# First expert stage of a two-layer MoE kernel: row gathers paced by their own landings, and TensorE waiting tile by tile

## What is computed

```
x = x + 0.5 * ffn(layernorm(x))      # 8 experts, top 2, 1,024 slots per expert
x = x + attention(layernorm(x))      # 16 heads of 8, linear attention with elu+1
x = x + 0.5 * ffn(layernorm(x))      # the same weights again

def ffn(x):
    scores = softmax(x @ wg); topv, topi = top_k(scores, 2)
    disp[topi, pos] = x                      # rows to the slots of their experts, at most 1,024 each
    h = relu(disp @ w1 + b1); y = h @ w2 + b2    # 128 -> 512 -> 128 for each expert
    return sum_k gate_k * y[topi_k, pos_k]
```

## Time and profile before

| | |
|---|---|
| median of 3 runs | 514.09 us |
| lowest, highest | 510.62, 518.35 us |
| the profiled execution | 502.3 us |
| its span, first to last instruction | 500.6 us |
| mean granted TensorE clock in it | 0.848 |
| PE busy | 350.9 us (70%) |
| DVE busy | 354.0 us (71%) |
| POOL busy | 272.6 us (54%) |
| gathers of the first expert stage | 64, from 50.1 to 147.1 us |

### The profile page before, as it was taken

The page is one execution under the profiler, slowest core; times in us unless marked ns, Lnnn a source line. Parts: engine busy times, 40 slices in busy tenths (PEclk is TensorE's granted clock), DMA queues, the critical chain, the costliest instruction groups (busy, mean ns, idle before and its releaser), DMA issues.

```text
span 500.6 us, 6027 instructions
## 1 busy us (share of the span) xinstructions
PE 350.9 (70%) x1710; PEld 286.2 (57%) x1710; DVE 354.0 (71%) x1084; ACT 235.4 (47%) x431; POOL 272.6 (54%) x302
## 2 busy tenths in 40 slices
PE   6913589999999256869777684000789999999400
PEld 6903368888887135748665563000768888888300
DVE  6898379998887545779886586300068989999573
ACT  3687156766666044453642543200057766666200
POOL 8000766766653556666666356777303677777720
PEclk9999999999999867795775896555689999999955
DMA  8930315676663411111111011111401223321489
GB/s 233 353 109 1 111 43 194 196 228 222 211 215 128 126 43 42 43 44 42 45 49 48 29 37 54 53 56 56 163 9 50 87 89 90 91 61 43 139 316 284
DMA packets 45216, 55.48 MB, mean 111 GB/s; under 512 B 6694, under 2 KB 28736, under 8 KB 45184
## 3 DMA queue, kind: packets, MB, share of 16 engines
q1 hardware_dynamic: 32304, 35.40, 21.4%
q0 software_dynamic: 8512, 17.60, 12.1%
q10 hardware_dynamic: 4368, 2.10, 1.4%
HBM read 25.98 MB, written 29.10 MB: 110 GB/s over the span
## 4 chain that ended last, share of the span: by engine, by line
PE 40%; POOL 17%; DMA 12%; issue 11%; DVE 6%; another core or an unknown queue 2%; ACT 1%; POOLq 0%; DVEq 0%; SPq 0%; ACTq 0%
POOL xs_dram L838 8%; DMA yg<-y_dram,slot 6%; PE psum L1041 5%; PE psum L1054 5%; PE psum L1037 5%; PE psum L1052 5%; PE psum L1053 5%; POOL yt_dram L996 5%; PE psum L1038 5%; POOL xg L1010 3%; PE psum L1063 2%; PE psum L1024 2%; DMA ring<-yt_dram 2%; POOL yg L1250 2%
## 5 line engine op out<-in xcount | busy, mean ns | idle before, releaser
L1104 ACT ACTIVATE hf<-psum,bcol 128x512 f32<-128x512 f32 x128 | 88.4, 693 | 65.2 <-PE psum L1041 42.0
L1010 POOL DMA_INDIRECT xg<-xn_dram,gidx x64 | 66.3, 1035 | 68.8 <-POOLq L1671 38.2
L996 POOL DMA_INDIRECT yt_dram<-y_sb,target x64 | 71.6, 1119 | 53.3 <-DVE y_sb L1157 30.9
L1141 DVE TENSOR_TENSOR hl<-hf,hh 128x512 fp32r<-128x512 f32 x128 | 87.8, 698 | 5.0 <-ACT hh L1106 1.4
L1250 POOL DMA_INDIRECT yg<-y_dram,slot x64 | 61.5, 961 | 48.6 <-DMA yg<-y_dram,slot 24.0
L838 POOL DMA_INDIRECT xs_dram<-xns,place x64 | 62.2, 971 | 35.0 <-issue 19.3
L1130 DVE TENSOR_TENSOR xl<-psum,xh 128x512 fp32r<-128x512 f32 x32 | 21.9, 683 | 51.8 <-ACT xh L1089 51.8
L1037 PE MATMUL psum<-xh,wres 128*128 128x512 f32 x128 | 54.0, 422 | 3.8 <-ACT xh L1089 3.8
L1052 PE MATMUL psum<-hh,wres 128*128 128x512 f32 x128 | 52.8, 412 | 0.0
L1041 PE MATMUL psum<-xl,wres 128*128 128x512 f32 x128 | 51.6, 403 | 0.8 <-DVE xl L1130 0.7
L1038 PE MATMUL psum<-xh,wres 128*128 128x512 f32 x128 | 51.2, 400 | 0.0
(11 more groups left out here) (239 smaller groups left out, 751.6 us busy)
## 6 DMA issues: line engine op xcount, KB each, us to landing
yt_dram<-zeros SPq DMA_DIRECT2D x24, 256.0 KB
ring<-yt_dram SPq DMA_DIRECT2D x24, 256.0 KB
xs_dram<-zeros SPq DMA_DIRECT2D x16, 288.0 KB
xg<-xs_dram SPq DMA_DIRECT2D x16, 288.0 KB
wexp_raw<-in_L_ffn_w SPq DMA_DIRECT2D x16, 256.0 KB, 6.0
y_dram<-y_rows_out SPq DMA_DIRECT2D x16, 256.0 KB
x_sb<-in_L_attn_x SPq DMA_DIRECT2D x8, 256.0 KB, 3.9
xn_dram<-xns SPq DMA_DIRECT2D x8, 256.0 KB, 5.8
```

What stands on the lines that cost most here:

```text
L996: gp.indirect_dma_start(out=yt_dram, out_offset=bass.IndirectOffsetOnAxis(ap=target[:, j:j + 1], axis=0), in_=self.y_sb[:, s % YG, t], in_ ...
L1010: gp.indirect_dma_start(out=self.xg[:, s % 4, t], out_offset=None, in_=xn_dram, in_offset=bass.IndirectOffsetOnAxis(ap=gidx[:, j:j + 1], a ...
L1104: one = nc.scalar.activation(self.hf[:, c], bank[1 + c][:], ACT.Relu, bias=bcol[:, at:at + 1])
L1141: dve.tensor_tensor(self.hl[:, s % 2, c], self.hf[:, c], self.hh[:, s % 2, c].bitcast(F32), ALU.subtract).then_inc(hl_ready[c], 1)
```

## The change

Two edits in `Experts`, both for the first expert stage only:

- POOL: gather number i (i = 4s + t) no longer waits for PE's products. From i = 2 on it waits for the landing of gather i - 2. From chunk 4 on, the first gather of a chunk waits before that for `xT_ready >= s - 3`, which says that PE has transposed chunk s - 4 and its buffer is free. Each gather counts on the semaphore of its tile number, `gathered[t]`, no longer on that of its buffer.
- PE: the first transpose of a chunk waits for tile 0, and each of the other three for its own tile.

Everything else (the order of the instructions on every engine, the buffers, the stores and zero fills of SP) stays as it is.

```diff
             def gpsimd(self, gp):
                 for s in range(NSB):
+                    if s >= 4:
+                        gp.wait_ge(xT_ready, s - 3)
                     for t in range(GT):
-                        if s == 2 and t == 0:
-                            gp.wait_ge(xT_ready, 1)
-                        elif s == 2:
-                            gp.wait_ge(h_ready[t - 1], 1)
-                        elif s >= 3:
-                            older, c = divmod(HC * (s - 3) + 2 + t, HC)
-                            gp.wait_ge(h_ready[c], older + 1)
+                        i = GT * s + t
+                        if i >= NARROW:
+                            gp.wait_ge(gathered[(i - NARROW) % GT], landings(i - NARROW))
                         j = GT * self.order[s] + t
                         gp.indirect_dma_start(out=self.xg[:, s % 4, t], out_offset=None, in_=xn_dram,
-                                              in_offset=bass.IndirectOffsetOnAxis(ap=gidx[:, j:j + 1], axis=0)).then_inc(gathered[s % 4], 16)
+                                              in_offset=bass.IndirectOffsetOnAxis(ap=gidx[:, j:j + 1], axis=0)).then_inc(gathered[t], 16)
 
             def tensor(self, pe):
                 b = self.b
 
                 def turn(s):
                     if self.f == 0:
-                        pe.wait_ge(gathered[s % 4], 64 * (s // 4 + 1))
+                        pe.wait_ge(gathered[0], landings(GT * s))
                     else:
                         pe.wait_ge(slot_rows_in[s % XG], 16 * (s // XG + 1))
                     if b + s > 0:
                         pe.wait_ge(xl_ready, b + s)
                     for t in range(GT):
+                        if self.f == 0 and t > 0:
+                            pe.wait_ge(gathered[t], landings(GT * s + t))
                         last = nc.tensor.transpose(bank[0][:, t * P:(t + 1) * P], self.xg[:, s % (4 if self.f == 0 else XG), t, 0:C], ident[:])
                     last.then_inc(xT_ready, 1)
```

## The result

| | before | changed |
|---|---|---|
| first measurement, median (range, runs) | 512.23 us (506.31 to 518.35, 6) | 519.66 us (514.16 to 526.33, 6) |
| first measurement, ratio | | 1.034, 95% interval 1.024 to 1.043 |
| again, on a chip whose runs lie closer together | 490.55 us (486.7 to 492.94, 11) | 506.27 us (505.68 to 508.0, 6) |
| again, ratio | | 1.033, 95% interval 1.029 to 1.037 |
| span of a profiled execution | 500.6 us | 512.4 us; again 504.3 us |

The kernel became slower, by 3.3% or 15.7 us in the second measurement, which is the closer one and the one I rely on. I had forecast +6 us (1.3%), so the difference is two to three times the forecast. That the predicted absolute time of 520 us lies on the first measurement's median is luck: the runs there spread over 12 us for either kernel, and the two medians differ by 7.4 us only.

What follows compares the result with a forecast made beforehand. It took PE, at 6.37 us a chunk, to bound the first expert stage before; 5.8 us from chunks 5 to 15 plus 0.5 us at the start gave +6.3 us (+1.3%), hence 520 us, range 511 to 528.

Steps and rivals of the forecast that it cites:

- the three waits on PE: First expert stage, PE: the added waits per chunk, one per transpose, cost zero; 22 us if each cost 0.48 us.
- the second wait at the head of a four: POOL, first gather of a chunk from chunk 4 on: its additional buffer wait costs 0.48 us.
- The zero net of the first chunk: Stage start: gather 3 0.9 us late, three transposes run 0.8 us early, so zero net.
- a gather that falls into a burst costs the chain about 0.75 us: POOL's gathers beside SP's stores and fills: a landing in such a burst delays the chain about 0.75 us.
- one hit per chunk from a fixed phase: Expert stage: one gather pair per chunk, the middle one, falls into SP's burst, making 6.9 us a chunk.
- my 1.83: POOL's gathers in quiet traffic: 1.83 us from an instruction's end to the start that waits for its landing.
- that 0.53: Chunks 5 to 15: each pays 6.9 - 6.37 = 0.53 us beyond PE's time.
- my 6.9: POOL's gather chain per chunk: 6.03 quiet + 0.75 for one hit + 0.12 for longer instructions = 6.9 us.
- 5.8 us of the sum: Chunks 5 to 15 together: 11 chunks at 0.53 us each, 5.8 us of the +6.3 us.
- rival 2: Expert stage: two burst hits a chunk, 7.3 to 7.8 us each, +11 to +16 us, 525 to 530 us; chance 0.25.
- the phase argument: Expert stage: with gathers as the bound, burst and gathers keep a fixed phase, so only the middle pair is squarely hit.
- 0.5 us from the first five chunks: Stage start, chunks 0 to 4: delays of PE add 0.5 us in all.

Runs made afterwards that it cites:

- e4_tile_waits: Kernel before with only PE's edit: old gather pacing, 16 semaphores, each transpose waiting for its own tile; 489.88 us, ratio 1.000.
- e7_one_input: Changed kernel with the VectorE subtractions L1141 and L1126 replaced by copies of their first operand; 7.39 us a chunk, no whole-kernel time given.
- e2_yt_late: Changed kernel with only the yt_dram zero fills moved behind the last store; 515.69 us in one run, 7.14 us a chunk.
- e8_yt_late_again: Changed kernel with only the yt_dram zero fills moved behind the last store, profiled a second time; 515.22 us in one run, 7.24 us a chunk.
- e5_pacing_only: Changed kernel with PE waiting for all four tiles before a chunk's first transpose; 504.12 us, ratio 1.027 to the kernel before.
- e3_three_back: Changed kernel with each gather waiting for the landing three back instead of two; 490.41 us against 489.63 before, ratio 1.002.
- e1_fills_late: Changed kernel with all zero fills of xs_dram and yt_dram moved behind the last y_dram store; 520.11 us in one run, 6.37 us a chunk.

## Why the prediction was wrong

**What held.** PE bounds the stage before, with no wait from chunk 4 on; the change puts POOL's chain of landings in its place; the three waits on PE are free (e4_tile_waits); the second wait at the head of a four costs POOL about 0.48 us, visible again as idle times of 0.72 to 0.84 us at the heads of four chunks (two others have 0.65 and 0.44), where POOL else idles 0.30 us; the loss goes to the end almost undiminished. The sign and the mechanism were right. The zero net of the first chunk was nearly so: its first product comes 0.55 us later than before (59.35 against 58.80), the single transposes giving 0.71 (e4_tile_waits) and the later landing taking more.

**The term that was too small in the cadence: "a gather that falls into a burst costs the chain about 0.75 us", once a chunk.** I priced a hit where SP had issued one store and one fill, and counted one hit per chunk from a fixed phase. The changed kernel has 29 gathers from chunk 4 on that a landing released. Worked out from its timeline, from the end of a gather's instruction to the start of the one two later: a third take the quiet 1.74 to 1.90 us (my 1.83), the mean is 2.61, and 20 of the 29 take more than 2.0, up to this one:

```profile
102.66 0.94 POOL L1008 DMA_INDIRECT xg<-xn_dram,gidx  x1 [0.53 <-DMA xg<-xn_dram,gidx]
104.44 0.94 POOL L1008 DMA_INDIRECT xg<-xn_dram,gidx  x1 [0.84 <-issue]
108.71 0.94 POOL L1008 DMA_INDIRECT xg<-xn_dram,gidx  x1 [3.32 <-DMA xg<-xn_dram,gidx]
```

The gather of 102.66 ended at 103.60, and its successor started at 108.71: 5.11 us, 3.3 above the quiet value. SP had issued a step's store and fills from 101.94 to 103.86. So hits are more frequent than one a chunk (20 in 12 chunks) and can cost four times what I took. The error is not large in itself, 0.35 to 0.7 us on a chunk of 6.9, but only what exceeds PE's 6.37 us counts, and that 0.53 became 0.88 and 1.21. Besides, some of PE's stalls bring the half clock on top, which the forecast had at no place. That raises a chunk from my 6.9 to 7.25 and 7.58 us, and 5.8 us of the sum to 9.7 and 13.3. It is the place in the forecast that rival 2 stood for ("two hits a chunk", decided from 7.26 us on), with a chance of 0.25. Its total, +11 to +16 us, holds the measured 15.7, in part by luck: it has 0.5 us for the start, and the first profile's 7.25 us a chunk lies just below its bound.

Against the phase argument speaks the spread itself: a chunk takes 6.4 to 8.8 us in the changed kernel, from one to the next, so burst and gathers keep no fixed phase.

The Trainium skill, DMA: Bandwidth & Descriptors, "Latency and other measured facts", has 2 us of HBM latency under high load against 0.2 in the mean. I had set it aside in favour of the one row that I could read; the traces agree with its order of size for single landings (up to 3.3 us late, the late ones of the 29 by 1.1 us in the mean), and the mean of the 29, 0.8 us late, lies between the two.

**The term that was too small at the start: "0.5 us from the first five chunks".** It was 3.75 to 4.25 us in the two profiles of the changed kernel, and 0.8 to 5.4 over all five with that start. Two things are missing in it. First, I took the gather's instruction at 0.95 us there, since those of before last that long while VectorE is busy. But before, the VectorE instructions beside gathers 8 to 13 start or end within 0.04 us of the gathers' starts and take the delay themselves (L1141 lasts 0.75 us there instead of 0.69); the paced gathers start where a landing puts them; at 60.01, 63.85, 65.32 and 66.98 that was beside an L1126 or L1141, and four instructions together got 2.2 us longer, in the one phase that has no run-ahead. With shorter VectorE instructions chunk 3 is 0.4 us late (e7_one_input), but with few instructions stretched by chance it is 0.8 us late as well (e2_yt_late). Second, I gave a stall its own length. Stalls of 2.8 us in 3.8 cost another 1.6 us, because PE then ran at the half clock for some 3 us.

The Trainium skill, SBUF — State Buffer, "Who interferes with whom", says that a VectorE instruction with two inputs in SBUF contends with a GpSimd instruction that reads SBUF and not with one that only writes; by that rule the gather, which reads its indices from SBUF, can be stretched, and the traces agree so far (1.96 us beside L1126, 0.94 alone). They show the same beside a cast with one input in SBUF (1.15 us beside L1134), so they don't single out the two inputs.

**Left open.** Why single landings are 2 to 3 us late: in the case above DMA moved only 25 GB/s from 107 to 108 us, with the gather still not landed, so the bytes in front of it are not the whole account, and halving the fills (e2_yt_late, e8_yt_late_again) took away 0.4 us of the chunk at most, not half of the loss. That all fills together take the chain from 6.41 us a chunk to 7.25 and more is shown, by which path is not; and what makes landings late beside the store alone, 6.41 instead of the 6.03 of the quiet rows, was not tried. Nor is it shown what decides whether TensorE's clock falls behind a stall, or whether the tile waits make the changed kernel a little slower by splitting PE's stall, as the middle of e5_pacing_only would have it.

## What to carry to other kernels

A wait for the landing of the transfer n back turns a throughput into a latency: the rate becomes n per landing time, and it must be compared with the need at the late landings and not at the quiet ones. Here two under way need 6.03 us a chunk in the quiet and 7.25 to 7.6 us in traffic against a need of 6.37; three under way fit (e3_three_back) at no cost. Price such a wait from the spread of landings in the same traffic, and where only a calmer stretch can be read, take its late landings as the floor. At the start of a stage, where nothing has run ahead, each delay counts in full and more than once, since a stall can bring TensorE down to its lower clock.

## What the runs showed of the hardware

- An indirect DMA's instruction on GpSimd that starts while VectorE runs an instruction whose inputs are all in SBUF (the subtractions L1126 and L1141 with two, the cast L1134 with one) ends 0.80 to 0.92 us after that one; up to 1.98 us instead of 0.94. Beside VectorE instructions that read PSUM (L1130, L1165) it lasts 0.94 to 1.05 us.
- Waits of 0.41, 1.43 and 1.00 us close behind each other were followed by a granted clock of 0.61 and matmuls 0.43 instead of 0.23 us apart for about 3 us; waits of 2.08 and 0.84 us in e1_fills_late by a clock of 0.50 for some 5 us. Waits of 1.40, 0.32 and 1.41 us in e8_yt_late_again did not. Later in the stage a single stall was followed by it in some executions (1.97 us in the second profile of the changed kernel, 2.71 us in e2_yt_late) and not in others (2.16 us in the first profile).
- 768 KB of fills issued just ahead of a gather made it land about 1.2 us later (54.51 against 53.34 for the gather that waits for it).
